# Layer 2 of a graph network kernel takes its one-hots from memory and raises to a power for two groups at once; layer 0 copies turned one-hots ahead of its exponential

## The chip, the cores and the metric

One NeuronCore of a Trainium2 chip runs the whole kernel in one launch. The time is the device time of that launch in microseconds, the median of several runs.

## The reference, cut to what matters

Four graph layers run one after the other on 6250 nodes with 106,250 edges (a source, a target and a weight each), with a normalisation ahead of each. Layer 0 is an attention over hyperedges, with sums over edges at one end and then at the other; layer 1 an MLP on both ends of an edge; layer 2 a gated message passing; layer 3 graph attention in two rounds. Layer 2 is the one that the change touches most:

```python
src_h = feat @ W_src + b_src
dst_h = feat @ W_dst + b_dst
se = src_h[edge_src]
de = dst_h[edge_dst]
h = gelu(se @ W1a + de @ W1b + b1)
h = gelu(h @ W2 + b2)
msg = _layernorm(h @ W3 + b3, ln_g, ln_b)
gate = jax.nn.sigmoid(gelu(se @ Wg1a + de @ Wg1b + bg1) @ Wg2 + bg2)
msg = gate * msg
upd = jax.ops.segment_sum(msg, edge_dst, num_segments=N)
return upd @ W_out + b_out
```

## The kernel before

The edges are sorted once by the block of 128 nodes that their target (and in a second order, their source) lies in. They are padded to 928 tiles of 128 edges; four tiles are a **group**, and there are NG = 232 groups. Every pass over the edges is a software pipeline over groups. Each engine has its own program, written out in full: in iteration j of `sweep`, a step with lag n works on group j - n, and `turn(j, u, n)` gives that group if it exists. The engines meet only through semaphores, whose counts are worked out in advance (`RAISED` says how often a group raises each of them in a pass). Nothing schedules: the order in the text is the order on the engine. `ORDER = "abafcdee"` lists the passes: a and b in the first half of layer 0 (b is its sum pass), a and f in the second half, c for layer 1, d for layer 2, e twice for layer 3. Between passes all engines meet (`meet`).

Rows of node tables are gathered by indirect DMAs that POOL issues, four per group (`rows_po`, L585). Sums over edges into nodes are matmuls with **one-hots**: a 128x128 matrix with a one where an edge belongs to a node of its block. Their turned form (transposed) spreads node values over edges. The one-hots of a group are 128x512 comparisons on VectorE (`onehot_ve`, L891, from `iof` and `LOW`, both in SBUF); `turn_pe` (L910) transposes them on TensorE, and `turned_ac` (L916) copies the result from PSUM. Pass b writes the source side's one-hots to memory, pass f the target side's, in 768 columns a group: 256 hold the turned form in bf16, 512 the plain form. Layer 1 (pass c) and f read them back on SP's queue in one transfer a group (`stream_sp`); layer 2 before the change builds its own. The sum of a group is read by `add_ve` (L884, L887), which adds two blocks to the accumulators at addresses that it takes from block numbers in memory: `blocks` (L565) loads them into registers on the queue of the engine.

Layer 2, pass d, for group g in iteration j of each engine: sv matmuls of the turned one-hots (lag 2, L1332), z on VectorE (lag 3, L1204), transposes and Gelu (lag 4, L1324, L1281, L1283), W2 (lag 5, L1318), Gelu (L1276) and the gate's product and sum (L1227, L1242), then W3 (lag 6, L1307), z3 = product + b3 (L1213), batch statistics (L1233, L1249), variance + eps (L1254), the gate's tanh (L1271); POOL raises the variance to -0.5 (`d_po`, L1187, 128x4); lag 7: VectorE makes scale and bias (L1221, L1222, L1237) and ScalarE scales z3 (L1293, four times); lag 8: sums (L897); lag 9: adds. The reciprocal root stands on POOL ahead of the gathers of iteration j:

```python
for j in range(NG + 6):
    if j >= 6:
        ...
        po.tensor_tensor(dRS[:, g % 2, :], dVE[:, g % 2, :], dPW, ALU.pow).then_inc(S.rs, 1)
    if j < NG:
        ...
        rows_po(po, p, 0, tab[256], dG, j)
```

## Time and profile before

| | us |
|---|---|
| median of 3 runs | 11944.33 (11938.95 to 11951.59) |
| profiled execution | 11948.37 |
| its span | 11946.6 |

Busy shares of the span: PE 73%, DVE 69%, POOL 66%, ACT 43%. The profile gives in its parts: the busy time of each engine, the same in slices of time, DMA queues, a chain of what ended last, and groups of instructions by line. A row of a group has the engine and line, what is written and read, the count after x, the busy time in us, the mean length of one in ns, and the idle time of the engine just before, with what released it ("issue": nothing that the profile shows). A row of the timeline has the start in us, the length in us, the engine and line. A row of the windows has the stretch, its length, then for PE, PEld, DVE, ACT and POOL the busy time with the number of instructions, then the granted clock of TensorE as a share of full speed, the DMA share, and GB/s. PE is the matmul side of TensorE, PEld its weight loads, DVE VectorE, ACT ScalarE, POOL GpSimd.

### The profile page before, as it was taken

To read this page: it belongs to the slowest core of one execution; us is meant where nothing else is said; L and a number is where in the kernel's file an instruction comes from. 1 tells how busy PE (TensorE), PEld (TensorE's weight loads), DVE (VectorE), ACT (ScalarE), POOL (GpSimd) and SP (SyncE) were. 2 spreads that over 40 slices of the span, in tenths; PEclk is the share of its full clock that TensorE was granted. 3 is DMA by queue.
4 is the path that set the end of the run, shared out by engine and by line. 5 is a ranking of instruction groups with operands and counts; after the bars stand their busy time and mean duration, and the time that the engine had idled before them with its cause. 6 is when DMAs were issued, how large, how long until landed. Compare 5 with 4: busy or idle time off the path is not lost. (4 is left out here: it accounts for less than half of the span.)

```text
span 11946.6 us, 191958 instructions
## 1 busy us (share of the span) xinstructions
PE 8708.9 (73%) x51661; PEld 7108.5 (60%) x51661; DVE 8225.6 (69%) x30197; ACT 5137.3 (43%) x14885; POOL 7921.6 (66%) x7887
## 2 busy tenths in 40 slices
PE   7797877788885887666654555689997677767776
PEld 5676777677764777544443555577776455444554
DVE  7655888755556777655554222499998688878888
ACT  3454444433333444322221111266665466646665
POOL 2333777677774777677764777288885577747775
PEclk7766677655555666665656666799999665666656
DMA  1112222255552222377763444233332444434443
GB/s 16 7 19 38 54 54 54 56 126 126 128 129 58 54 54 54 97 202 203 202 168 93 131 132 131 79 89 88 88 88 68 124 135 134 136 105 136 134 135 114
DMA packets 612550, 1206.43 MB, mean 101 GB/s; under 512 B 185426, under 2 KB 298544, under 8 KB 610992
## 3 DMA queue, kind: packets, MB, share of 16 engines
q0 software_dynamic: 282368, 575.57, 22.4%
q1 hardware_dynamic: 288768, 523.78, 13.7%
q10 hardware_dynamic: 40368, 94.82, 2.1%
q8 instruction: 452, 7.41, 0.3%
q14 instruction: 594, 4.87, 0.1%
HBM read 958.79 MB, written 234.74 MB: 100 GB/s over the span
## 5 line engine op out<-in xcount | busy, mean ns | idle before, releaser
L585 POOL DMA_INDIRECT WK<-tab,IDX x4640 | 4608.4, 993 | 1736.2 <-issue 1391.7
L1388 POOL DMA_INDIRECT B<-tab,IDX x1856 | 1774.1, 956 | 844.8 <-issue 503.7
L897 PE MATMUL PS<-WK 128*128 128x129 f32 x5568 | 1140.8, 368 | 628.4 <-ACT WK L1134 500.5
L897 PEld LDWEIGHTS PS<-WK 128*128 128x128 f32 x5568 | 992.4, 267 | 719.4 <-ACT WK L1134 550.4
L1407 DVE TENSOR_REDUCE WK<-PS 128x4 f32<-128x1024 f32 x928 | 1131.4, 1220 | 184.0 <-PE PS L1533 181.9
L1518 ACT ACTIVATE B<-B 128x33 f32<-128x33 f32 x5568 | 1211.2, 308 | 7.9
L585 POOL DMA_INDIRECT H<-tab,IDX x928 | 901.9, 972 | 345.8 <-issue 256.2
L816 ACT ACTIVATE WK<-WK 128x128 f32<-128x128 f32 x1856 | 592.6, 390 | 1242.1 <-DMA WK<-tab,IDX 1230.0
L1566 PEld LDWEIGHTS PS<-B,H 128*128 128x128 f32 x3712 | 815.4, 329 | 273.9 <-issue 268.1
L1566 PE MATMUL PS<-B,H 128*128 128x132 f32 x3712 | 874.7, 428 | 78.5 <-DVE ACC L1420 78.3
L1533 PE MATMUL PS<-B 27*128 27x512 bf16 x1856 | 729.8, 505 | 118.8 <-DVE WK L1407 114.3
L453 POOL DMA_INDIRECT pieces<-WK,B x208 | 342.4, 1646 | 703.3 <-ACT WK L441 405.4
L845 PE MATMUL PS<-B 128*128 128x130 f32 x3712 | 797.2, 383 | 1.5 <-DVE B L776 1.5
L860 PEld LDWEIGHTS PS<-WK,B 128*128 128x128 f32 x3712 | 661.6, 267 | 176.0 <-issue 173.7
L860 PE MATMUL PS<-WK,B 128*128 128x2 f32 x3712 | 642.1, 295 | 128.6 <-DVE WK L773 127.5
L1120 DVE TENSOR_TENSOR WK<-PS,WK 128x512 f32<-128x512 f32 x232 | 160.5, 692 | 816.1 <-DMA WK<-tab,IDX 816.1
L845 PEld LDWEIGHTS PS<-B 128*128 128x128 f32 x3712 | 708.8, 283 | 2.4 <-DVE B L776 2.3
L645 PE MATMUL PS<-B,WT 128*15 128x512 bf16 x464 | 268.3, 578 | 569.6 <-ACT B L667 399.7
L387 PEld LDWEIGHTS PS<-B,WK 128*128 128x128 f32 x3328 | 530.9, 252 | 183.2 <-issue 181.4
L387 PE MATMUL PS<-B,WK 128*128 128x64 f32 x3328 | 529.5, 336 | 121.6 <-ACT WK L441 115.3
L1134 ACT ACTIVATE WK<-WK 128x512 f32<-128x512 f32 x232 | 146.6, 632 | 1028.3 <-DVE WK L1120 1028.3
L838 PE MATMUL PS<-WT,B 128*128 128x128 bf16 x1856 | 228.4, 262 | 451.9 <-ACT B L821 426.8
(426 smaller groups left out, 20454.5 us busy)
## 6 DMA issues: line engine op xcount, KB each, us to landing
H<-onehots SPq DMA_DIRECT2D x232, 768.0 KB
B<-onehots SPq DMA_DIRECT2D x232, 384.0 KB
onehots<-B ACTq DMA_DIRECT2D x232, 384.0 KB
WK<-onehots SPq DMA_DIRECT2D x232, 384.0 KB
WK<-tab,IDX POOLq DMA_INDIRECT x4640
onehots<-WK SPq DMA_DIRECT2D x232, 256.0 KB
onehots<-B SPq DMA_DIRECT2D x232, 128.0 KB
B<-tab,IDX POOLq DMA_INDIRECT x1856
```

The lines of the kernel that those rows point to most:

```text
L387: mm = pe.matmul(PS[:, 4 + x % 2, 64 * (t // TC):64 * (t // TC) + 64], OHL[x % 2][:, t, :], PROD[x % 2][:, t, :, :].rearrange("p i w -> p ...
L453: po.indirect_dma_start(out=recd[o], out_offset=bass.IndirectOffsetOnAxis(ap=ROWI[:, o, 2 * k + q:2 * k + q + 1], axis=0), in_=OUT[x % 4][ ...
L585: po.indirect_dma_start(out=G[:, g % n, k, :], out_offset=None, in_=table, in_offset=bass.IndirectOffsetOnAxis(ap=IDX[:, idx, t:t + 1], ax ...
L816: i = ac.activation(aXR[:, r % 4, k, :], aN1[:, 128 * k:128 * k + 128], ACT.Identity, bias=aG[:, r, k, 128:129])
L845: mm = pe.matmul(aAG(r, k // 2), aOH[:, r, k, :], aR[:, r % 2, k, 0:130], start=k % 2 == 0, stop=k % 2 == 1)
L860: mm = pe.matmul(as2[:, k, :], aOT[:, r % 4, 128 * k:128 * k + 128], aY[:, r % 2, k // 2, 1:3], start=True, stop=True)
L897: mm = pe.matmul(AG(r, k // 2), OH[:, r, k, :], R[:, r % 2, k, 0:129], start=k % 2 == 0, stop=k % 2 == 1)
L1388: po.indirect_dma_start(out=eG[:, g % 4, k, :], out_offset=None, in_=tab[TW3], in_offset=bass.IndirectOffsetOnAxis(ap=IDX[:, o, t:t + 1], ...
L1407: ve.tensor_reduce(eM2[:, g, b:b + 2, 2 * i:2 * i + 2, 1] if isinstance(g, int) else eM2[:, bass.ds(g, 1), b:b + 2, 2 * i:2 * i + 2, 1].re ...
L1518: i = ac.activation(eR[:, q, k, 33 * h:33 * h + 33], eG[:, r, k, 33 * h:33 * h + 33], ACT.Copy, scale=eEX[:, r, 4 * k + h:4 * k + h + 1])
L1533: mm = pe.matmul(PS[:, b + h, :], eSEL[:, b + h, :], eET[:, r, 512 * i:512 * i + 512], start=True, stop=True)
L1566: mm = pe.matmul(eAG(k // 2), eSTo[:, r, k // 4, 128 * (k % 4):128 * (k % 4) + 128], eR[:, r % 2, k, 0:132], start=k % 2 == 0, stop=k % 2 ...
```

## The change

Layer 2 no longer builds its one-hots. Pass f has left them in memory, and SP streams them in two transfers a group, into four buffers each (`d_sp`): the turned form as it is read by ScalarE, which widens it from bf16 to f32 (lag 1, where it copied from PSUM before), and the plain form six groups later, for the sums. VectorE's `onehot_ve` and TensorE's `turn_pe` are gone from the pass. POOL raises to the power for two groups in one instruction (128x8), at every second iteration. Scale, bias and the scaling move from lag 7 to 8, the sums from 8 to 9, the adds from 9 to 10; some small buffers are deeper. In pass b, ScalarE's two copies of the turned one-hots (group j - 1) stand ahead of the exponential (group j - 3).

```diff
-    "d": dict(oh=1, pt=1, ot=1, sv=1, z=1, zt=1, h1=1, mm=1, h2=1, p3=1, gp=1, gl=1, th=1, z3=1, bn=1, mv=1,
+    "d": dict(ot=1, sv=1, z=1, zt=1, h1=1, mm=1, h2=1, p3=1, gp=1, gl=1, th=1, z3=1, bn=1, mv=1,
...
-KEPT = {"a": 0, "b": 48, "f": 16, "c": 16, "d": 0, "e": 32}
+KEPT = {"a": 0, "b": 48, "f": 16, "c": 16, "d": 16, "e": 32}
...
             def body(j, u):
-                if f := turn(j, u, 3):
-                    g, r = f
-                    ac.wait_ge(S.p2, at.p2 + g + 1)
-                    ac.wait_ge(S.r, at.r + g - 3)
-                    ac.activation(bEX[:, r % 4, :], bDD[:, r % 2, :], ACT.Exp).then_inc(S.ex, 1)
                 if f := turn(j, u, 1):
                     g, r = f
                     kept(ac, 1, g, r)
                     ac.wait_ge(S.pt, at.pt + g + 1)
                     ac.activation(bTBt[r % 4], PS[:, r % 2, 0:256].bitcast(BF16), ACT.Copy).then_inc(s_kt, 1)
                     turned_ac(ac, at, g, r, bOT, r % 2)
+                if f := turn(j, u, 3):
+                    g, r = f
+                    ac.wait_ge(S.p2, at.p2 + g + 1)
+                    ac.wait_ge(S.r, at.r + g - 3)
+                    ac.activation(bEX[:, r % 4, :], bDD[:, r % 2, :], ACT.Exp).then_inc(S.ex, 1)
                 if f := turn(j, u, 2):
...
-        dOH, dOT, dR, dH2, dZ3 = room(fd, 8, 4, 128), room(fd, 2, 512), room(fd, 2, 4, 133), room(fd, 512), room(fd, 2, 512)
-        dBN, dMV = room(fd, 2, 4, 6), room(fd, 2, 4, 2)
-        dVE, dRS, dTH, dGW, dGT, dNM, dGL = (room(fd, 2, 4) for _ in range(7))
-        dPW = room(fd, 4)
+        dSTt = [room(fd, 256).bitcast(BF16) for _ in range(4)]
+        dSTo = room(fd, 4, 4, 128)
+        dOT, dR, dH2, dZ3 = room(fd, 2, 512), room(fd, 2, 4, 133), room(fd, 512), room(fd, 3, 512)
+        dBN, dMV = room(fd, 2, 4, 6), room(fd, 4, 4, 2)
+        dTH, dGW, dNM, dGL = (room(fd, 2, 4) for _ in range(4))
+        dVE, dRS, dGT = (room(fd, 4, 4) for _ in range(3))
+        dPW = room(fd, 2, 4)
         hf, xf = flat(H[:, :, :]), flat(X[:, :, :])
...
             for j in range(NG + 6):
-                if j >= 6:
-                    g = j - 6
+                g = j - 6
+                if g % 2 == 1 and g > 0:
                     po.wait_ge(S.mv, at.mv + g + 1)
-                    po.wait_ge(S.r, at.r + g - 1)
-                    po.tensor_tensor(dRS[:, g % 2, :], dVE[:, g % 2, :], dPW, ALU.pow).then_inc(S.rs, 1)
+                    po.wait_ge(S.r, at.r + g - 3)
+                    h = g % 4 - 1
+                    po.tensor_tensor(dRS[:, h:h + 2, :], dVE[:, h:h + 2, :], dPW, ALU.pow).then_inc(S.rs, 2)
                 if j < NG:
                     po.wait_ge(S.z, at.z + j - 3)
                     rows_po(po, p, 0, tab[256], dG, j)
@@ -1193,8 +1197,8 @@
...
-                z, w, l, f = turn(j, u, 6), turn(j, u, 7), turn(j, u, 5), turn(j, u, 0)
-                if x := turn(j, u, 9):
+                z, w, l = turn(j, u, 6), turn(j, u, 8), turn(j, u, 5)
+                if x := turn(j, u, 10):
                     add_ve(ve, at, 0, *x, AGd)
...
-                    qz = rz % 2
+                    qz, vz, sz = rz % 2, rz % 4, gz % 3
                     ve.wait_ge(S.p3, at.p3 + gz + 1)
-                    ve.wait_ge(S.rs, at.rs + gz - 1)
-                    ve.wait_ge(S.r, at.r + gz - 1)
-                    ve.tensor_tensor(by128(dZ3[:, qz, :]), by128(PS[:, 5, :]),
+                    ve.wait_ge(S.rs, at.rs + gz - 3)
+                    ve.wait_ge(S.r, at.r + gz - 2)
+                    ve.tensor_tensor(by128(dZ3[:, sz, :]), by128(PS[:, 5, :]),
                                      b3b.unsqueeze(1).broadcast_to([128, 4, 128]), ALU.add).then_inc(S.z3, 1)
                 if w:
                     gw, rw = w
-                    qw = rw % 2
-                    ve.wait_ge(S.rs, at.rs + gw + 1)
+                    qw, vw = rw % 2, rw % 4
+                    ve.wait_ge(S.rs, at.rs + gw - gw % 2 + 2)
                     ve.wait_ge(S.ag, at.ag + gw - 1)
                     ve.wait_ge(S.r, at.r + gw - 1)
-                    ve.tensor_copy(dR[:, qw, :, 128], dGT[:, qw, :])
-                    ve.tensor_tensor(dGW[:, qw, :], dGT[:, qw, :], dRS[:, qw, :], ALU.mult).then_inc(S.gw, 1)
+                    ve.tensor_copy(dR[:, qw, :, 128], dGT[:, vw, :])
+                    ve.tensor_tensor(dGW[:, qw, :], dGT[:, vw, :], dRS[:, vw, :], ALU.mult).then_inc(S.gw, 1)
                 if l:
                     gl, rl = l
                     ve.wait_ge(S.h1, at.h1 + gl + 1)
@@ -1230,11 +1234,11 @@
                 if z:
...
-                if f:
-                    onehot_ve(ve, at, 0, *f, dOH)
...
-                    ac.wait_ge(S.r, at.r + g - 1)
+                    ac.wait_ge(S.mm, at.mm + g - 1)
...
-                    turned_ac(ac, at, *f, dOT, 0)
-                if f := turn(j, u, 7):
+                    g, r = f
+                    streamed(ac, p, g, r)
+                    ac.wait_ge(S.sv, at.sv + g - 1)
+                    ac.activation(dOT[:, r % 2, :], dSTt[r % 4], ACT.Copy).then_inc(S.ot, 1)
+                if f := turn(j, u, 8):
                     g, r = f
                     q = r % 2
                     ac.wait_ge(S.nm, at.nm + g + 1)
                     ac.wait_ge(S.ag, at.ag + g - 1)
                     for k in range(4):
-                        i = ac.activation(dR[:, q, k, 0:128], dZ3[:, q, 128 * k:128 * k + 128], ACT.Identity,
+                        i = ac.activation(dR[:, q, k, 0:128], dZ3[:, g % 3, 128 * k:128 * k + 128], ACT.Identity,
                                           bias=dNM[:, q, k:k + 1], scale=dGW[:, q, k:k + 1])
                     i.then_inc(S.r, 1)
             meet(ac)
-            sweep(7, body)
+            sweep(8, body)
+
+        def d_sp(sp, p):
+            at, ring = raised_before(p)
+            for j in range(NG + 6):
+                if j < NG:
+                    sp.wait_ge(S.ot, at.ot + j - 3)
+                    sp.dma_start(dSTt[j % 4], oht[0][j, :, 0:256].bitcast(BF16)).then_inc(s_kd[j % 4], 16)
+                if j >= 6:
+                    g = j - 6
+                    sp.wait_ge(S.ag, at.ag + g - 3)
+                    sp.dma_start(dSTo[:, g % 4, :, :].rearrange("p k n -> p (k n)"), oht[0][g, :, 256:768]).then_inc(
+                        s_k0[g % 4], 16)
 
...
-                if f := turn(j, u, 1):
-                    turn_pe(pe, at, *f, upper(dOH), 0, 1)
-                if f := turn(j, u, 8):
-                    sum_pe(pe, at, *f, dOH, dR, AGd, 1)
+                if f := turn(j, u, 9):
+                    g, r = f
+                    pe.wait_ge(s_k0[r % 4], 32 * (NG // 4) + 16 * (g // 4 + 1))
+                    sum_pe(pe, at, g, r % 4, dSTo, dR, AGd, 1)
...
             meet(sp)
+            d_sp(sp, 5)
             meet(sp)
```

The rows that follow are the engines' programs in order: source line, operation, written and read tensor, shape. Lines behind the change are shifted by four or more. On VectorE in layer 2, before, from the variance + eps (L1254) of one iteration into the next:

```order
L1254 TENSOR_SCALAR WK<-WK 128x4
L891 TENSOR_TENSOR WK<-iof,LOW 128x512
L565 TENSOR_LOAD BLK
L884 ISA
L884 TENSOR_TENSOR ACC<-ACC,PS 128x129
L887 ISA
L887 TENSOR_TENSOR ACC<-ACC,PS 128x129
L1204 TENSOR_TENSOR H<-PS,H 128x1024
L1213 TENSOR_TENSOR WK<-PS,WT 128x512
```

And after:

```order
L1258 TENSOR_SCALAR WK<-WK 128x4
L565 TENSOR_LOAD BLK
L884 ISA
L884 TENSOR_TENSOR ACC<-ACC,PS 128x129
L887 ISA
L887 TENSOR_TENSOR ACC<-ACC,PS 128x129
L1208 TENSOR_TENSOR H<-PS,H 128x1024
L1217 TENSOR_TENSOR WK<-PS,WT 128x512
```

Only the comparison that makes the one-hots (L891) is gone; the load of block numbers (L565) and the address arithmetic (ISA) for the add stay between the variance and the add.

On POOL in layer 2, with the semaphores that an instruction waits for, before:

```order
L1187 TENSOR_TENSOR WK<-WK 128x4 [waits p_r,p_mv]
L585 DMA H<-tab,IDX 128x256 [waits p_z]
L585 DMA H<-tab,IDX 128x256 x3
L1187 TENSOR_TENSOR WK<-WK 128x4 [waits p_r,p_mv]
L585 DMA H<-tab,IDX 128x256 [waits p_z]
L585 DMA H<-tab,IDX 128x256 x3
```

And after:

```order
L1191 TENSOR_TENSOR WK<-WK 128x8 [waits p_r,p_mv]
L585 DMA H<-tab,IDX 128x256 [waits p_z]
L585 DMA H<-tab,IDX 128x256 x3
L585 DMA H<-tab,IDX 128x256 [waits p_z]
L585 DMA H<-tab,IDX 128x256 x3
```

The power stands ahead of every second group's four gathers, with twice the columns.

On ScalarE in pass b, one iteration and a half, before (L970 is the exponential, L975 and L916 the copies, L649 the copy of the bit form):

```order
L970 ACTIVATE WK<-WK 128x4 [waits p_r,p_p2]
L975 ACTIVATE B<-PS 128x512 [waits p_pt,k_kept1]
L916 ACTIVATE WK<-PS 128x512 [waits p_sv,p_pt]
L649 ACTIVATE B<-PS,WT 15x512 [waits k_bits]
L970 ACTIVATE WK<-WK 128x4 [waits p_r,p_p2]
```

And after, where L970 is the copy and L976 the exponential:

```order
L970 ACTIVATE B<-PS 128x512 [waits p_pt,k_kept3]
L916 ACTIVATE WK<-PS 128x512 [waits p_sv,p_pt]
L976 ACTIVATE WK<-WK 128x4 [waits p_r,p_p2]
L649 ACTIVATE B<-PS,WT 15x512 [waits k_bits]
L970 ACTIVATE B<-PS 128x512 [waits p_pt,k_kept0]
```

The exponential has moved from ahead of the two copies to behind them.

## Rows read from the trace of the kernel before

**Rows 1.** Windows inside pass b, layer 1 and layer 2.

```profile
2400.00:3600.00 1200.00, 1009.85 (x4684) 845.32 (x4683) 614.28 (x2454) 407.25 (x892) 928.26 (x892) 0.53 0.56 127
6450.00:7450.00 1000.00, 572.60 (x3986) 519.72 (x3982) 253.19 (x597) 125.72 (x199) 757.46 (x797) 0.69 0.45 131
7800.00:9100.00 1300.00, 1182.78 (x7295) 956.56 (x7296) 1234.90 (x4294) 857.33 (x1931) 1058.55 (x1074) 1.00 0.30 88
```

**Rows 2.** Groups of instructions of POOL in layer 2, 7800 to 9100 us.

```profile
L1187 POOL TENSOR_TENSOR WK<-WK 128x4 f32<-128x4 f32 x215 | 224.2, 1043 | 5.0
```

**Rows 3.** Timeline of POOL in layer 2, one group.

```profile
8400.00 1.04 POOL L1187 TENSOR_TENSOR WK<-WK 128x4 f32<-128x4 f32 x1
8401.23 1.02 POOL L585 DMA_INDIRECT H<-tab,IDX  x1 [0.19 <-issue]
...
8405.08 0.95 POOL L585 DMA_INDIRECT H<-tab,IDX  x1 [0.31 <-issue]
8406.07 1.04 POOL L1187 TENSOR_TENSOR WK<-WK 128x4 f32<-128x4 f32 x1
```

**Rows 4.** Timeline of DVE in layer 2, the same group time.

```profile
8400.27 0.68 DVE L1213 TENSOR_TENSOR WK<-PS,WT 128x512 f32<-128x512 f32 x1
8401.08 0.17 DVE L1221 COPY WK<-WK 128x4 f32<-128x4 f32 x1
...
8401.23 0.73 DVE L1227 TENSOR_TENSOR X<-X 128x512 f32<-128x512 f32 x1
...
8403.79 0.24 DVE L1254 TENSOR_SCALAR WK<-WK 128x4 f32<-128x4 f32 x1
8403.94 0.68 DVE L891 TENSOR_TENSOR WK<-iof,LOW 128x512 f32<-128x512 f32 x1
8404.55 0.29 DVE L884 TENSOR_TENSOR ACC<-ACC,PS 128x129 f32 x1
```

**Rows 5.** Timeline of PE and ACT in layer 2, the same time.

```profile
8399.92 1.16 PE L897 MATMUL PS<-WK 128*128 128x129 f32 x8 [0.51 <-ACT WK L1293]
8401.10 1.10 PE L1318 MATMUL PS<-X,WT 128*128 128x512 f32 x2
...
8402.24 0.69 ACT L1276 ACTIVATE WK<-PS,WT 128x512 f32<-128x512 f32 x1 [1.97 <-PE PS L1318]
...
8402.47 1.89 PE L1332 MATMUL PS<-B,WK 128*128 x8
...
8403.82 0.60 ACT L916 ACTIVATE WK<-PS 128x512 f32<-128x512 bf16 x1
...
8404.20 1.05 PE L1307 MATMUL PS<-WT,WK 128*128 128x128 f32 x8
...
8404.29 1.64 ACT L1293 ACTIVATE WK<-WK 128x128 f32<-128x128 f32 x4
```

**Rows 6.** Timeline of DVE at the end of layer 2's pass.

```profile
9149.54 0.29 DVE L884 TENSOR_TENSOR ACC<-ACC,PS 128x129 f32 x1 [0.54 <-issue]
...
9152.11 0.17 DVE L1221 COPY WK<-WK 128x4 f32<-128x4 f32 x1
...
9157.91 0.16 DVE L1221 COPY WK<-WK 128x4 f32<-128x4 f32 x1
```

**Rows 7.** The power at 49 columns, in the normalisations; shortest, median, longest in ns.

```profile
L546 POOL TENSOR_TENSOR WK<-WK x6: 8162/8194/8792, 1050.1 to 9245.0; 128x49 f32<-128x49 f32 x6
```

**Rows 8.** Groups of instructions in pass b, 2400 to 3600 us.

```profile
L585 POOL DMA_INDIRECT WK<-tab,IDX x892 | 928.6, 1041 | 272.0 <-issue 259.9 <-DVE WK L939 12.2
...
L645 PE MATMUL PS<-B,WT 128*15 128x512 bf16 x223 | 132.8, 595 | 163.2 <-ACT B L975 162.0
```

**Rows 9.** A ScalarE instruction that reads SBUF, in layer 1, from the groups of the page.

```profile
L1134 ACT ACTIVATE WK<-WK 128x512 f32<-128x512 f32 x232 | 146.6, 632 | 1028.3 <-DVE WK L1120 1028.3
```

**Rows 10.** Timeline of DVE and POOL in pass b, one gather and a multiplication.

```profile
2808.37 0.69 DVE L939 TENSOR_TENSOR WK<-WK 128x512 f32<-128x512 f32 x1
2808.52 1.37 POOL L585 DMA_INDIRECT WK<-tab,IDX  x1 [0.30 <-issue]
```

More of the change, by code:

```diff
@@ L1246, in body @@
                     ve.wait_ge(S.th, at.th + gz + 1)
-                    ve.tensor_scalar(dGT[:, qz, :], dTH[:, qz, :], 0.5, 0.5, ALU.mult, ALU.add)
+                    ve.tensor_scalar(dGT[:, vz, :], dTH[:, qz, :], 0.5, 0.5, ALU.mult, ALU.add)
                     for k in range(4):
-                        i = ve.bn_aggr(dMV[:, qz, k, :], dBN[:, qz, k, :])
+                        i = ve.bn_aggr(dMV[:, vz, k, :], dBN[:, qz, k, :])
                     i.then_inc(S.mm, 1)
@@ L1253, in body @@
                     ve.wait_ge(S.mm, at.mm + gz + 1)
-                    ve.tensor_scalar(dVE[:, qz, :], dMV[:, qz, :, 1], EPS, None, ALU.add).then_inc(S.mv, 1)
-                if f:
-                    onehot_ve(ve, at, 0, *f, dOH)
+                    ve.tensor_scalar(dVE[:, vz, :], dMV[:, vz, :, 1], EPS, None, ALU.add).then_inc(S.mv, 1)
             for i in range(NGR - 4, NGR):
@@ L1260, in d_ve @@
             meet(ve)
-            sweep(9, body)
+            sweep(10, body)
         def d_ac(ac, p):
```

6 lines of the change are left out of this document (3 added, 3 removed).

## The prediction

> **What bounds the kernel now.** I read the windows by stage first, to see which engines are full in the two stages that the change touches. In the part of layer 2 that lies between its ramps, 1300 us of it, PE is busy 1182.78, DVE 1234.90, POOL 1058.55, and the granted clock is 1.00 [rows 1]. Busy shares don't decide it there, since three engines are above 80%. So I read POOL's own timeline next. The reader is to see that a group takes five instructions in a fixed rhythm: the power at 8400.00, four gathers of which the first starts at 8401.23 and the last at 8405.08, the next power at 8406.07, with 0.19 to 0.31 us of idle time before a gather that only issue explains, and none before the power [rows 3]. The grouped row says the same of all of them: 215 powers of 1043 ns with 5.0 us idle ahead of them in total [rows 2]. POOL waits for nobody, so it is full, at a group time of (8406.07 - 8400.00) = 6.07; over the window, 1300 us hold 215 groups, 6.05 us each (6.06 by first and last start; I use 6.06).
>
> Two more loops are nearly as long. VectorE: the add of b3 ends at 8400.95, and the copy of the gate (L1221) starts at 8401.08, 0.04 after the power has ended (8400.00 + 1.04) and 0.13 after the add, where the following instructions start before their predecessor has ended [rows 3, 4]. So VectorE gives some 0.2 us a group to the power. ScalarE and TensorE: from the start of the first Gelu at 8402.24 to the end of the four scale instructions (8404.29 + 1.64) are 3.69 us; the sum matmuls then start (0.51 idle, released by that instruction), and 1.18 later the W2 matmul, which lasts 1.10 and releases the next Gelu [rows 5]. That is 3.69 + 0.06 + 1.18 + 1.10 + 0.04 = 6.07, the whole group time, but W2 also waits for VectorE's add, which ended only 0.15 before it started. All three loops move in step, and the one without slack is POOL's.
>
> In the first sum pass of layer 0, POOL is full as well: 892 gathers, 928.6 busy and 272.0 idle, of 1200 us [rows 8]. PE waits there 163.2 us for ScalarE's copy (L645), which costs nothing while POOL sets the pace.
>
> **Layer 2, the power for two groups.** One instruction on 128x8 takes the place of two on 128x4. The trace has this operation at two widths: 1043 ns for 4 columns [rows 2] and 8194 ns for 49 [rows 7]. The line through both is 0.41 us + 0.159 us a column, so 8 columns take 1.68 us. Bounds: proportional to the columns, 2 x 1.04 = 2.08; by the rate of the wide one with nothing fixed, 8 x 8194/49 = 1.34; and nothing but a fixed cost, 1.04. I take 1.68, since the two rows leave a fixed part of 0.4 and a much larger part per column. The Trainium skill (GPSIMD Engine Reference, section 3.1) puts an element of a two-input operation at about 2.6 cycles of that engine, which would make columns almost free, and 8 of them hardly dearer than 4; the two rows speak against it for a power, with 159 ns a column.
>
> POOL's two groups then are: power to first gather 1.23 + (1.68 - 1.04) = 1.87; the next three starts 3.85 later in all, as now; the second group without a power, four starts 1.25 apart, as in the pass of layer 1 where nothing else runs on POOL (797 instructions in 1000 us, [rows 1]); and 0.99 from the last gather to the next power [rows 3]. Sum 1.87 + 3.85 + 5.00 + 0.99 = 11.71, or 5.86 a group, 0.20 less than now.
>
> **Layer 2, the one-hots streamed.** VectorE loses L891, 0.68 us. I cost that at almost nothing. The instruction behind it, the add to the accumulator (L884), needs block numbers that the queue loads from memory, and the queue gets to them once L1254 is started: L1254 starts at 8403.79, L884 at 8404.55, 0.76 later, and L891 lies in that gap [rows 4]. The end of the stage shows the same iteration without L891, since no one-hots are left to build: the gap stays, L884 at 9149.54 with 0.54 of idle time that issue explains [rows 6]. Two whole iterations there without it, with VectorE never waiting for another engine, are 9157.91 - 9152.11 = 5.80 us [rows 6]. So VectorE's own loop is 5.80 to 5.85, before and after, and that is a floor.
>
> PE loses four transposes; they lie between L1307 and the sums, where it waits 0.51 for ScalarE anyway [rows 5], so nothing is gained. ScalarE copies from SBUF in place of PSUM: L1134, from SBUF, takes 632 ns [rows 9] against 0.60 for L916 [rows 5], so +0.04 in its loop. That loop without VectorE's hold on W2: W2 has started 0.02 after the sums' modelled end, while L1307 starts 0.16 ahead of the end of L1332 [rows 5], so some 0.18 of it is wait, and 6.07 - 0.18 + 0.04 = 5.93 bounds the loop from above; the same sum with the W2 matmul itself shortened by its cold start (its weights could load during the sums) is about 5.87, an estimate. I take 5.88 for the group: POOL's 5.86 and 0.02 for loops that touch, as now.
>
> The two streams per group go on SP's queue, 384 KB, as in layer 1, where the DMA share is 0.45 and the starts on POOL keep their 1.25 us [rows 1]. Layer 2 now has 0.30; with the stream it stays under 0.6. I cost it at nothing. Its cover: a transposed block is asked for when the copy four groups before it is done, about 17 us ahead. SP waits for the sums of group g-4 before the second form, and the next first form is queued behind that; the sums named are two iterations old by then, so it isn't late. The extra stage (sums one group later, adds one later) lengthens the end: one more power width, 0.64, and one more set of scale instructions, 1.64 [rows 5], some 2 us.
>
> Sum: 232 x (6.06 - 5.88) = 42 us, less 2 = 40 faster.
>
> **Layer 0, copies ahead of the exponential.** Nothing is added or removed. The copies no longer stand behind an exponential that waits for rows; PE's wait at L645 should go. The exponential now stands behind copies that wait for PE's transposes of two groups further on, but they are done about when the rows for it land. POOL's gathers are what all wait for, and I put the gain at 0. What could move is the lock in the next paragraphs, by up to 43 us either way.
>
> The sum is made against the profiled execution, 11948.4 us (span 11946.6): 11908.4. It is 4.0 above the median of 11944.33, so I predict 11905.
>
> **Rivals.**
> 1. The power costs in proportion, 2.08. POOL's pair is 12.11, as now; time 11944 + 2 = 11946. For it: the rows of 49 columns may be of another rhythm than short ones. Also here: the change doesn't reach the path at all.
> 2. The power's second half is nearly free (1.04 to 1.34). POOL falls to 5.54 to 5.69, and VectorE's 5.80 to 5.85 decides: 232 x 0.23 - 2 = 51 faster, 11893. VectorE idle would vanish and POOL show waits for L1254.
> 3. The port. In the pass of layer 0 a gather that starts 0.15 after a multiplication with two SBUF inputs (L939) takes 1.37 in place of 0.95 [rows 10]. In layer 2 the like instruction (L1227) and the first gather both start at 8401.23 [rows 3, 4], and that gather takes 1.02: a tie that POOL wins now. If VectorE wins it after the change, each pair costs 0.5 more, 0.25 a group, 58 us: 11963. Against it: both are still released by the end of the same power. The Trainium skill (SBUF - State Buffer, who interferes with whom) says that a VectorE instruction with two SBUF inputs and a GpSimd instruction that reads SBUF exclude each other, and whichever starts first holds the port. By that rule, the trace agrees in layer 0 (1.37 for 0.95), and the one-hots gone would be locks gone; in layer 2 the row shows no gather that L891 delays, so I count no gain. In layer 0, mean gathers of 1041 ns against 757.46/797 = 950 in layer 1 [rows 1, 8] cost 4 x 0.09 x 232 = 84 us; another phase could halve or add half of that, 42: 11863 or 11947.
> 4. The other side: TensorE's clock. Granted 1.00 in layer 2 at a busy share of 91%, but 0.53 in layer 0's sum pass at 84% and 0.69 in layer 1 [rows 1]. PE's 1182.78/215 = 5.5 us a group, less 0.4, is 5.1; at 0.69 it would be 7.4 and PE the bound: 232 x 1.34 = 310 slower, 12255. It decides from a clock of about 0.87 down (5.1/5.88). Against it: what is removed is small, and the shorter group packs the rest as densely.
>
> **How the numbers follow.** The case of the sum (5.86 to 5.93 a group, 11894 to 11917): 0.60. Rival 1: 0.12. Rival 2: 0.08. Lock in layer 2: 0.06. Clock: 0.03. Layer 0 off by more than 20 us, on top of the sum: 0.11, half each way. The range 11880 to 11946 takes in the sum's case with its neighbours, rivals 1 and 2, and leaves out the port, the clock and half of layer 0's. A measurement here tells 0.2%, 24 us, from no change, so below 11920 counts as faster: 0.60 x 0.95 + 0.08 + 0.05 = 0.70; slower (above 11968): the clock, part of the port, 0.06; the same: 0.24.
>
> **What the profile after would show.** Power instructions 116 of 1.68 us; starts of powers 11.7 to 11.8 apart; gathers in the second group 1.25 apart; an idle of about 0.6 ahead of L884 with "issue"; PE still waiting for ScalarE ahead of the sums; clock 1.00; in layer 0 no wait at L645 and the same 5.38 a group. I am wrong if the power's width is off by more than 0.2, if a gather in layer 2 is over 1.2 us, or if layer 0's mean gather moves by more than 20 ns.

## The result, and the profile after

The changed kernel takes 11871.4 us (median of 4 runs, 11866.9 to 11892.34) against 11941.85 (4 runs of the kernel before beside them), a ratio of 0.9943 (95% interval 0.9926 to 0.996): 70 us faster, where 39 were forecast. Its profiled execution took 11892.34 (span 11890.6), its slowest run; the kernel before had 11948.4 there.

The windows of the changed kernel, inside pass b, layer 1 and layer 2 (length, then PE, PEld, DVE, ACT and POOL busy, granted clock, DMA share, GB/s), answer to [rows 1]:

```profile
2400.00:3550.00 1150.00, 967.32 (x4550) 791.84 (x4550) 597.67 (x2387) 422.23 (x867) 886.05 (x867) 0.56 0.54 129
6450.00:7450.00 1000.00, 574.75 (x4006) 516.96 (x4004) 254.40 (x600) 126.36 (x200) 755.90 (x802) 0.70 0.46 132
7800.00:9000.00 1200.00, 1032.13 (x6120) 847.74 (x6120) 1051.18 (x3876) 801.10 (x1837) 961.18 (x919) 1.00 0.52 157
```

Layer 2 holds 204 groups in 1200 us, 5.88 us each, at a clock of 1.00. But look at the second window too: layer 1, which the change doesn't touch, has 802 gathers in its 1000 us, where it had 797.

Groups of instructions of the changed kernel in layer 2, 7800 to 9000 us, beside [rows 2, 4, 5]:

```profile
L585 POOL DMA_INDIRECT H<-tab,IDX x817 | 792.1, 970 | 236.9 <-issue 236.9
L1191 POOL TENSOR_TENSOR WK<-WK 128x8 f32<-128x8 f32 x102 | 170.3, 1670 | 2.2
L884 DVE TENSOR_TENSOR ACC<-ACC,PS 128x129 f32 x204 | 59.2, 290 | 110.9 <-issue 110.9
```

The power for two groups takes 1670 ns (1.68 forecast). The idle time ahead of L884, where the one-hots lay, is 110.9/204 = 0.54 us. POOL waits for no engine.

The timeline of POOL there, beside [rows 3]:

```profile
8401.48 1.67 POOL L1191 TENSOR_TENSOR WK<-WK 128x8 f32<-128x8 f32 x1
8403.34 1.02 POOL L585 DMA_INDIRECT H<-tab,IDX  x1 [0.19 <-issue]
8404.66 0.95 POOL L585 DMA_INDIRECT H<-tab,IDX  x1 [0.30 <-issue]
```

From the power to the first gather 1.86 (1.87 forecast), then eight gathers; the first is 1.02 long as before, so the tie with VectorE's product is still POOL's. The sixth is another matter. Over the pass it takes 1022 ns in the mean, where the undisturbed ones take 950: VectorE's product of the other group (L1231) starts 0.2 to 0.6 us ahead of it, mostly 0.5. (In the second execution of this kernel, below, it is the second gather behind the power in place of the sixth, with 1021 ns.) 14 gathers of the pass are over 1.2 us, 11 of them sixth ones; before there was one in all. The longest, with its product:

```profile
8715.40 0.69 DVE L1231 TENSOR_TENSOR X<-X 128x512 f32<-128x512 f32 x1
...
8715.58 1.34 POOL L585 DMA_INDIRECT H<-tab,IDX  x1 [0.30 <-issue]
```

Groups of the changed kernel in pass b, 2400 to 3550 us, beside [rows 8]:

```profile
L585 POOL DMA_INDIRECT WK<-tab,IDX x867 | 887.7, 1024 | 264.3 <-issue 253.9 <-DVE WK L939 10.4
...
L645 PE MATMUL PS<-B,WT 128*15 128x512 bf16 x217 | 127.5, 588 | 0.0
```

The wait at L645 is gone, and the mean gather is 1024 ns where it was 1041.

Where the time went is best read pass by pass. Each number below is the time in us from the start of the first gather of a pass to the start of its last (928 gathers), taken from the records of one profiled execution; the last column is from the first gather of layer 2 to the end of the execution.

| kernel | a | b | a again | f | c (layer 1) | d (layer 2) | d to the end |
|---|---|---|---|---|---|---|---|
| before | 1186.3 | 1248.3 | 1191.4 | 1226.3 | 1164.2 | 1398.0 | 4194.6 |
| changed | 1173.7 | 1230.5 | 1189.5 | 1234.6 | 1157.4 | 1359.3 | 4160.2 |
| difference | -12.6 | -17.8 | -1.9 | +8.3 | -6.8 | -38.7 | -34.4 |

Layer 2 gave what was forecast (-39). The other 31 us are 37 from passes a, b and c, of which the change touches only b, and 2 from the repetition of a, less 8 that f takes back. Behind layer 2 some of it is lost again: the gathers of layer 3 (L1388, L1405 changed) have a median of 955 ns for 952, and are 2545.6 us from first to last for 2539.1. (In this execution the part ahead of the first gather took 10 us longer, 1148.3 for 1138.0, and 1127.5 in another of the same kernel; it drifts.)

### The profile page after: what moved, and what is told of

It is laid out like the page before. It is cut to its first block and busy times, and to the rows that moved or that the text cites. A ratio compares the mean times of both kernels' runs of the same rounds, so it can differ in the third digit from the quotient of the medians.

```text
span 11890.6 us, 189871 instructions
## 1 busy us (share of the span) xinstructions
PE 8648.0 (73%) x50733; PEld 7039.9 (59%) x50733; DVE 8092.2 (68%) x29965; ACT 5150.1 (43%) x14885; POOL 7848.2 (66%) x7771
## 5 line engine op out<-in xcount | busy, mean ns | idle before, releaser
L1405 POOL DMA_INDIRECT B<-tab,IDX x1856 | 1782.6, 960 | 840.2 <-issue 504.3
L1120 DVE TENSOR_TENSOR WK<-PS,WK 128x512 f32<-128x512 f32 x232 | 160.5, 692 | 811.9 <-DMA WK<-tab,IDX 808.6
L387 PEld LDWEIGHTS PS<-B,WK 128*128 128x128 f32 x3328 | 538.5, 254 | 177.9 <-issue 175.7
L645 PE MATMUL PS<-B,WT 128*15 128x512 bf16 x464 | 267.8, 577 | 395.2 <-ACT B L667 392.5
L995 PEld LDWEIGHTS PS<-B,WK 128*128 128x128 f32 x1856 | 378.9, 303 | 265.9 <-issue 265.9
```

Source lines behind the costliest of these rows:

```text
L387: mm = pe.matmul(PS[:, 4 + x % 2, 64 * (t // TC):64 * (t // TC) + 64], OHL[x % 2][:, t, :], PROD[x % 2][:, t, :, :].rearrange("p i w -> p ...
L995: mm = pe.matmul(PS[:, 2 + r % 2, k:k + 1], bOT[:, r % 2, 128 * k:128 * k + 128], B2[:, bass.ds(v[k // 2], 1)], start=True, stop=True)
L1405: po.indirect_dma_start(out=eG[:, g % 4, k, :], out_offset=None, in_=tab[TW3], in_offset=bass.IndirectOffsetOnAxis(ap=IDX[:, o, t:t + 1], ...
```

## The experiments

Two questions: which part of the change gives what, and why do gathers outside layer 2 get shorter? For the second, the records of pass b give a first theory. In the kernel before, 306 gathers start less than 0.7 us after the start of a VectorE instruction with two SBUF operands (L891, L939). Grouped by that offset, they are longer than the undisturbed ones by these medians:

| offset, ns | 68 | 137 | 237 | 338 | 436 | 545 | 645 |
|---|---|---|---|---|---|---|---|
| before: number, ns longer | 26, 493 | 112, 425 | 35, 324 | 36, 226 | 33, 125 | 31, 16 | 33, 0 |
| changed: number, ns longer | 17, 490 | 98, 429 | 30, 338 | 35, 222 | 35, 136 | 41, 17 | 59, 0 |

So such a gather is held until 0.56 us after that instruction's start: in each column but the last, offset and lengthening of the kernel before add up to 561 to 564 ns. I call the sum of these lengthenings the **lock** of a pass: 84 us in pass b before, 73 changed.

Each set of experiments ran on a chip of its own, with the kernel before run in between; ratios are to that. "Pass b 1233.3" means the span of gathers as in the table above.

### The parts of the change

**The changed kernel again**, no edit.

> The changed kernel once more, to see how far its runs lie apart and what the passes outside the change do. Both theories: 65 to 75 us faster than before (ratio 0.994). Theory A (the order of the copies in layer 0 gives what layer 2 doesn't): pass b is 25 to 35 us shorter than before, and the first pass a is as before. Theory B (no edit gives it; POOL's gathers in passes that the change doesn't touch are shorter by chance, by the port and by a base length that differs between executions): the shortening is spread over passes a, b, f and c, 5 to 15 us each, with both signs from run to run.

11869.43 us, ratio 0.9937 (0.9923 to 0.995), which is 75 us; the medians are 86 apart. Pass b 1237.3, layer 2 1358.7, c 1157.3, and the first pass a 1165.2: all of it is there again. Theory A is out as it stands (a is 21 us shorter, b only 11), and so is B's "by chance": c has the same 7 us.

**Layer 2 alone**: pass b's order put back.

```diff
+                (exponential, lag 3)
                 (copies of the turned one-hots, lag 1)
-                (exponential, lag 3)
```

> Layer 2 as changed, layer 0's pass b in the old order. A: 39 us faster than before (0.9967), layer 2 at 5.88 us a group. B: the same 65 to 75 us as the full change.

11889.13, ratio 0.995 (0.9936 to 0.9964): 60 us. Layer 2 1358.6. Passes a and c are as short as in the changed kernel (1168.3, 1157.5), so they come with layer 2's part of the change.

**The order in pass b alone**: the same edit the other way, in the kernel before.

> Only the order of ScalarE's copies and exponential in pass b. A: 25 to 35 us faster (0.9975), with the mean gather of pass b down from 1041 ns by 30 ns. B: within 10 us of before.

11931.74, ratio 0.9981 (0.9972 to 0.999), 23 us faster. Pass b 1233.3 for 1248.3, with 69 us of lock for 84 and a mean gather of 1026 ns for 1042, half of what A forecast; the other passes are within 6 us of before. The forecast gain of 0 is refuted.

**The stream without the pair**: one power of 128x4 for each group, the rest of layer 2 as changed, pass b as before.

```diff
-                if g % 2 == 1 and g > 0:
+                if g >= 0:
...
-                    po.tensor_tensor(dRS[:, h:h + 2, :], dVE[:, h:h + 2, :], dPW, ALU.pow).then_inc(S.rs, 2)
+                    po.tensor_tensor(dRS[:, g % 4, :], dVE[:, g % 4, :], dPW[:, 0, :], ALU.pow).then_inc(S.rs, 1)
```

> Layer 2 with streamed one-hots and the later stages, but the power for one group at a time, 128x4; layer 0 in the old order. POOL then has five instructions a group again and sets 6.05 us a group: within 5 us of before by the mechanism of the prediction (power is the whole gain). The rival, that VectorE's one-hots or TensorE's transposes held the loops: 5.9 us a group, 35 us faster.

11998.55, ratio 1.0037 (1.0024 to 1.0051): slower than before. Layer 2 took 1424.9, 27 more than before. Its timelines of POOL and VectorE show the prediction's third rival at work, on the fourth gather of a group:

```profile
8406.80 1.42 POOL L585 DMA_INDIRECT H<-tab,IDX  x1 [0.30 <-issue]
...
8406.71 0.69 DVE L1230 TENSOR_TENSOR X<-X 128x512 f32<-128x512 f32 x1
```

The product starts 0.09 ahead of the gather, and the gather is 0.47 longer, 0.56 in all, as in pass b. 42 of the 232 fourth gathers, 18 in 100, take over 1.1 us. The power is held in the same way: 33 of 231 take more than 1.1 us, up to 1.57, where none did before. Gathers are 17 us longer in sum and powers 9.5, which is the 27. The rhythm of layer 2 decides whether a product falls ahead of a gather or a power; in the changed kernel it is one gather of a pair's eight, at a cost of some 8 us in the pass.

**The pair without the stream**: one-hots built by VectorE and turned by TensorE as before, the power for two groups.

```diff
+                if f:
+                    ve.tensor_tensor(dOH[:, g % 9, :, :], io4, low(0, g), ALU.is_equal).then_inc(S.oh, 1)
...
-                    streamed(ac, p, g, r)
-                    ac.activation(dOT[:, r % 2, :], dSTt[r % 4], ACT.Copy).then_inc(S.ot, 1)
+                    turned_ac(ac, at, *f, dOT, 0)
```

> Layer 2 with the power for two groups, but one-hots still built by VectorE and turned by TensorE (in 9 buffers, z3 in another place in memory); layer 0 in the old order. If the power is what layer 2 gained, and L891 lies in the shadow of the load of block numbers, layer 2 is at 5.88 us a group as with the streams, and the whole some 60 us faster than before, as the kernel with both parts of layer 2. Rival, that both parts are needed: VectorE with L891 is over its loop and layer 2 stays at 6.0 us or more.

11910.57, ratio 0.9967 (0.9955 to 0.9979), 39 us faster. Layer 2 1367.7; passes a and c short (1184.0, 1157.3). Its groups in layer 2, 7800 to 9000 us:

```profile
L585 POOL DMA_INDIRECT H<-tab,IDX x813 | 795.5, 979 | 235.7 <-issue 235.7
L1193 POOL TENSOR_TENSOR WK<-WK 128x8 f32<-128x8 f32 x101 | 168.7, 1670 | 2.2
L1264 DVE TENSOR_TENSOR WK<-iof,LOW 128x512 f32<-128x512 f32 x202 | 137.7, 682 | 0.0
```

The rival is out, and so is the forecast of 60 us: layer 2 runs at 5.92 us a group (powers 11.84 apart in the mean). POOL is full here too, and its gathers are 979 ns against 970 with the stream. So in layer 2 the pair is worth 30 us, and the stream 9 more by taking away one-hots that hold gathers (10 us of lock by L1264). The prediction had costed VectorE's 0.68 us at almost nothing; as VectorE time that is right.

### The 8 ns of passes a, b and c

The undisturbed gather is 952 ns in passes a, b and c before, and 944 in the changed kernel. This view groups the instructions of one line in layer 1, 6450 to 7450 us, shortest, median and longest in ns; before, then changed:

```profile
L585 POOL DMA_INDIRECT WK<-tab,IDX x797: 947/952/964, 6449.7 to 7449.3; - x200
```

```profile
L585 POOL DMA_INDIRECT WK<-tab,IDX x802: 940/944/965, 6449.8 to 7449.8; - x161
```

The repetition of a, and f, have 944 in both. 928 gathers by 8 ns are 7.4 us a pass, 22 for the three. On the usual chips all kernels with the power of 128x8 have 944 there, those with 128x4 have 952. The first idea was POOL's program, which is 113 rows shorter with the pair.

**Padding**: 116 writes of one column (128x1) on POOL behind layer 2, in the changed kernel and in the kernel before.

```diff
             d_po(po, 5)
             meet(po)
+            for _ in range(116):
+                own(po, "po", po.memset(WT[:, 1399:1400], 0.0))
```

> The changed kernel with 116 small memsets on POOL, in a stretch after layer 2 where POOL is idle, so that its program is as long as before the change. Theory P (the length of a gather on POOL, 944 or 952 ns in passes that the change doesn't touch, goes with where POOL's program lies or how long it is): the first pass a, b and c go back to 952 ns a gather, and the whole is 20 to 35 us slower than the changed kernel. Rival: it stays at 944 ns and the time is the same.

> The kernel before with the same 116 memsets. Theory P: the length of the program is another one again, so the gathers may go to 944 ns in pass a, b and c (20 to 35 us faster) or stay; the rival: 952 ns and the time of before.

Changed and padded: 11877.9, ratio 0.9936 (0.9923 to 0.9949), still 944 ns. Before and padded: 11949.55, 1.0003 (0.9994 to 1.0012), still 952.

**Padding in place**: in the changed kernel, such a write behind two waits long met, where each second power stood.

```diff
+                elif g >= 0:
+                    po.wait_ge(S.mv, at.mv + g)
+                    po.wait_ge(S.r, at.r + g - 3)
+                    own(po, "po", po.memset(WT[:, 1399:1400], 0.0))
```

> What it is: the changed kernel, in which POOL gets in every other group of layer 2, where the power of one group stood before, a write of one column (128x1) of an unused tile behind two waits that have long been met. POOL's program is then 4,179 rows long where before has 4,174 and the changed kernel 4,061, each row of layer 2 at about the place it has in before. Theory P (the undisturbed gather of passes a, b and c takes 944 ns in place of 952 because of the length of POOL's program or of the place of its instructions): it is 952 ns here again, and passes a, b and c are 5 to 8 us longer each than in the changed kernel. Rival Q (it is something that the 128x8 power itself brings, or its tiles): 944 ns stays.

11878.71 (2 runs), ratio 0.9935 (0.9912 to 0.9958), still 944. Length and place in POOL's program are not it.

**Two narrow powers** in place of the wide one, tiles, waits and streams as changed.

```diff
-                    po.tensor_tensor(dRS[:, h:h + 2, :], dVE[:, h:h + 2, :], dPW, ALU.pow).then_inc(S.rs, 2)
+                    po.tensor_tensor(dRS[:, h, :], dVE[:, h, :], dPW[:, 0, :], ALU.pow).then_inc(S.rs, 1)
+                    po.tensor_tensor(dRS[:, h + 1, :], dVE[:, h + 1, :], dPW[:, 1, :], ALU.pow).then_inc(S.rs, 1)
```

> What it is: the changed kernel with two powers of 128x4 one behind the other on POOL, every second group, in place of one of 128x8; tiles, waits, streams and order as in the changed kernel. Settles more of where the shorter undisturbed gather of passes a, b and c (944 ns for 952) comes from: the padded kernels spoke against the length of POOL's program. If it comes with the instruction of 8 columns, the gather is 952 ns here, as in the kernel with one power per group; if it comes with what goes with pairing (tiles of four groups, one stage more in layer 2's sweep), it stays 944 ns. Layer 2: two powers are 2.09 us for 1.67, so 6.1 us per group for 5.88, the gathers of layer 2 from first to last about 1405 us and the whole about 11,920.

> Two powers of 128x4 one behind the other in place of one of 128x8, once more on another chip. In the first run the undisturbed gather of passes a, b and c was 952 ns (944 in the kernels with one 128x8 power on the same chip), and that of the passes behind layer 2 fell to 944. If that goes with the kernel, both are so here again; if it was that chip, a, b and c are 944 ns. Layer 2: about 1405 us from first gather to last, 6.1 us per group; the whole, with 8 ns more per gather in three passes, 11,920 to 11,945 us.

The first run fell on an odd chip (below), the second gave 11928.59, ratio 0.998 (0.9971 to 0.999), layer 2 1394.9, 10 us under its forecast. On both chips a, b and c have 952 ns, and the repetition of a and f 944. (On the odd chip the kernels with the power of 128x8 have 947 in all five of these passes, not the 944 that the second expectation gives them.) The second run, layer 1:

```profile
L585 POOL DMA_INDIRECT WK<-tab,IDX x797: 947/952/968, 6449.8 to 7449.5; - x200
```

So the 8 ns go with the kernel, not with the chip, and not with the deeper tiles or the later stages; nothing is left that differs but the form and number of the power instructions, which run after the passes in question. What carries it back to them isn't found. Layer 3, behind the powers, moves too, and not in step: a median of 952 before, 955 changed, 944 with two narrow powers.

### Taking the lock away

**One SBUF operand in pass b.** The one-hots and the product of 128x4x128 are made by four instructions each, with one SBUF operand and a number per partition.

```diff
-            ve.tensor_tensor(OH[:, r, :, :], io4, low(o, g), ALU.is_equal).then_inc(S.oh, 1)
+            for k in range(4):
+                i = ve.tensor_scalar(OH[:, r, k, :], iof[:, :], LOW[:, o, 4 * g + k:4 * g + k + 1], None, ALU.is_equal)
+            i.then_inc(S.oh, 1)
...
-                    ve.tensor_tensor(bR[:, q, :, 0:128], bG[:, r % 4, :, 0:128],
-                                     bEW[:, q, :].unsqueeze(2).broadcast_to([128, 4, 128]), ALU.mult).then_inc(S.r, 1)
+                    for k in range(4):
+                        i = ve.tensor_scalar(bR[:, q, k, 0:128], bG[:, r % 4, k, 0:128], bEW[:, q, k:k + 1], None, ALU.mult)
+                    i.then_inc(S.r, 1)
```

> The changed kernel, where in pass b VectorE makes the one-hots (L891) and the product with the weights (L939) by four instructions each that read one tensor from memory and take the other operand as a scalar per partition. If the exclusion between a VectorE instruction with two inputs from SBUF and a gather on POOL is what makes pass b's gathers 1030 ns long, they fall to 944 to 955 ns, the pass from 1235 to about 1165 us, and the kernel is 70 us faster than the changed one, 1.2% faster than before. The rival (memory traffic of the streams that pass b writes makes them long): 1020 to 1040 ns as now, no gain.

11803.71, ratio 0.9887 (0.987 to 0.9904). Pass b is 1163.0. Its timelines of POOL and VectorE, to set beside [rows 10]:

```profile
2807.61 0.96 POOL L585 DMA_INDIRECT WK<-tab,IDX  x1 [0.30 <-issue]
...
2807.47 0.87 DVE L942 TENSOR_SCALAR WK<-WK 128x128 f32<-128x128 f32 x4
```

The gather starts 0.14 after the product's first piece, as the one of [rows 10] did at 0.15 after the whole product, and is 0.96 long where that took 1.37. The same holds for all: 184 gathers of pass b start less than 0.5 us after the first of four such pieces, and in steps of 100 ns their medians are 0 to 37 ns over the undisturbed length (60 ns for the 32 that start 0.7 to 0.8 us after it). All gathers of the pass together are 5 us over it.

The pieces are also shorter than what they replace, 0.3 us for 0.69, so this run alone leaves open whether the second SBUF operand holds a gather or the length does. Layer 1 of the kernel before settles it. Its VectorE instruction L1120 has the length and width of the product, but one operand from PSUM and one from SBUF:

```profile
L1120 DVE TENSOR_TENSOR WK<-PS,WK 128x512 f32<-128x512 f32 x199 | 137.7, 692 | 696.5 <-DMA WK<-tab,IDX 696.5
```

113 gathers of that pass start less than 0.6 us after the start of one; in every step of 100 ns their median is 952, and the longest of all is 961. So length doesn't do it; two operands from SBUF do.

**The same with the old order**, exponential ahead of the copies.

> What it is: the kernel with one-input one-hots and products in the first sum pass of layer 0 (11,803.71 us, pass b 1163.0 us), with ScalarE's exponential back ahead of its copies of turned one-hots. Theory L (the order that the change gives ScalarE in that pass gains only by moving VectorE's two-operand instructions off the starts of the gathers): with no such instructions left the order is worth nothing: pass b 1163 us within 3 us, the whole 11,795 to 11,815 us. Rival S (the order shortens a chain that the gathers wait for, ring slots given back later in the old order): pass b 15 us or more longer, about 1178 us, and the whole about 11,820.

11801.44, ratio 0.9873 (0.9855 to 0.9892), pass b 1161.7. In pass b, 2400 to 3450 us:

```profile
L585 POOL DMA_INDIRECT WK<-tab,IDX x838 | 795.0, 949 | 255.4 <-issue 247.2 <-DVE WK L942 8.2
L645 PE MATMUL PS<-B,WT 128*15 128x512 bf16 x210 | 124.0, 591 | 109.3 <-ACT B L978 107.7
```

This separates the two things that the order did. PE's wait at L645 is back with 109 us, and the pass is no longer for it: that wait costs nothing. Without the lock the order is worth nothing, so its gain went through the lock, as theory L had it; rival S is out.

**One SBUF operand in all passes of layer 0**: also L755 and L776 in a, L654 and L1031 in f.

> What it is: the changed kernel with every one-hot and every product of 128x4x128 that VectorE makes out of two SBUF operands in layer 0 (L654, L755, L776, L891, L939, L1031) made by four instructions with one SBUF operand and a number per partition. In pass b alone this took the gathers' first-to-last from 1229.5 to 1237.3 us down to 1163.0. Theory L (the gathers of layer 0 lose their time above the undisturbed issue length to VectorE instructions with two SBUF operands that start in the same half microsecond): pass f (1229.6 to 1240.1 us in the changed kernels) falls to about 1160 as pass b did, pass a and its repetition lose their lock sums of 8 to 34 us, mostly in the first pass (1164 to 1182 down to about 1160), and the whole comes to 11,690 to 11,740 us, ratio to before about 0.980. Rival W (VectorE in pass a is busy 4.2 of 5.1 us per group; the four pieces cost about 0.25 us more than the one, twice, and VectorE becomes what the gathers wait for there): passes a and a2 get longer, above 1200 us each, and the whole is 11,750 or more. Rival N (in pass f it was something else, such as the table stream or the kept tiles): f stays at 1230 and the whole at about 11,780.

11802.75, ratio 0.9873 (0.9854 to 0.9892), no better. Pass f fell from 1235.2 to 1162.6 and the repetition of a from 1188.2 to 1180.0, but the first pass a went from 1164.2 to 1233.4. There, 1140 to 2373 us:

```profile
L585 POOL DMA_INDIRECT WK<-tab,IDX x919 | 868.3, 945 | 354.9 <-issue 219.9 <-DVE B L782 135.0
```

No gather is held, and POOL waits 135 us for the product instead: a gather needs its buffer back, and VectorE has it for longer. Some of that falls into idle time that was there anyway (357 us between the gathers in all, where it is 282 with only pass b's pieces), so 75 us of it are paid. Theory L held for pass f, rival W for the first pass a alone, rival N is out.

**One SBUF operand in b and f** (pass a as changed), and **in b, f and a's one-hots** (L755), each twice, since the first time fell on the odd chip.

> What it is: the changed kernel with the one-hots and products of the passes b and f of layer 0 (L891, L939, L654, L1031) made in four pieces with one SBUF operand each, and pass a as in the changed kernel. Making all of them so gave 11,802.75 us, no better than pass b alone (11,803.71), although pass f fell from 1235.2 to 1162.6 us: in that run's first pass a the gathers took 1233.4 us where 1164.2 stood, with 135 us of waits for VectorE's product. Theory W (that was VectorE, busy 4.2 of 5.1 us per group of pass a, on which the eight pieces add 0.5 us): with pass a left alone both gains add up: b and f about 1163 us each, pass a 1164 to 1182, its repetition 1190, the whole about 11,735 us (11,720 to 11,755). Rival M (the length of the first pass a moves for a cause of its own, from run to run, and the one-input pieces of passes b and f bring it on): a is 1210 us or more here too, and the whole is near 11,780.

> The kernel with one-input pieces in passes b and f once more. In its first run the chip was one on which the kernel before itself took 15,087.74 us (11,941 to 11,958 elsewhere), its engines standing for about 4.5 us at every second group of pass a with what the trace calls remote; that run can't speak of the gathers' locks. On a chip where before takes about 11,950 theory W stands as written: b and f about 1163 us each, the whole about 11,735 us (11,720 to 11,755). Rival M: the first pass a at 1210 us or more, the whole near 11,780.

> What it is: as the kernel with one-input pieces in passes b and f, and in pass a the one-hots (L755) too in four pieces, the product (L776) left in one. The one-hots carry most of pass a's lock (11 to 20 us of 16 to 30). Theory W: VectorE gets 0.25 us of work per group more in place of 0.5, which it has room for: no 100 us of waits for it, the first pass a and its repetition come to 1165 to 1175 us, the whole is 10 to 25 us under the kernel with b and f alone. Rival W2 (any added work on VectorE in pass a is paid, since its chain from a table row to the product is what gives the ring slot back): pass a 20 to 40 us longer than there, the whole no better or slower.

> The kernel with one-input pieces in passes b and f and for the one-hots of pass a once more, for the same reason. Theory W: the first pass a and its repetition 1165 to 1175 us, the whole 10 to 25 us under the kernel with b and f alone. Rival W2: pass a 20 to 40 us longer than there, the whole no better or slower.

On a usual chip, b and f give 11740.94, ratio 0.9827 (0.9813 to 0.9841): 1.7% under the kernel before and 1.1% under the changed one. a 1164.7, b 1163.0, f 1170.5, both forecast within 8 us. In pass f, 5000 to 6000 us, where the kernel before has gathers of 1024 ns in the mean:

```profile
L585 POOL DMA_INDIRECT WK<-tab,IDX x792 | 752.1, 950 | 248.9 <-issue 238.1 <-DVE WK L1037 10.8
```

With a's one-hots too it is 11750.98, ratio 0.9834 (0.9821 to 0.9847), no gain: the repetition of a gets shorter (1170.8 for 1189.8), the first pass longer (1193.8 for 1164.7), with the product left in one piece now holding 219 gathers for 30 us (5 gathers for 2 us with b and f alone). Making only one of two instructions harmless took lock away in the repetition (31 to 8 us) and brought more to the first pass, where the other now falls ahead of gathers. Of the two rival readings for pass a, W2 ("no better") came out, though by the lock and not by waits for VectorE: the idle time between the gathers is the same 282.5 us in both kernels.

**The odd chip.** There the kernel before took 15087.74 us, b and f 15763.45 (ratio 1.0446, 1.0422 to 1.047), b, f and a's one-hots 15752.96 (1.0439, 1.042 to 1.0459), the two narrow powers 15587.15 (1.033, 1.0303 to 1.0356). The list of waits of the b and f kernel in its first pass a there, 1146 to 2900 us (total, times, longest):

```profile
ACT B L823 <- remote: 518.1, 114, 16.4
DVE WK L725 <- remote: 504.7, 113, 7.0
```

VectorE and ScalarE stand 4.5 us at a time at every second group for something that the trace can't name; no list of waits elsewhere has that row. On this chip POOL isn't the bound, so its runs say nothing of the lock, and the numbers of the others don't hold there. What it is was not tried.

## Why the prediction was right and wrong

- **Layer 2, the power's width**: right. 1.68 was worked out from 4 and 49 columns, 1670 ns measured. Proportional cost (rival 1) and a free second half (rival 2) are out.
- **Layer 2, 5.88 a group**: right, 5.88, but in part by luck. POOL's own 5.86 was sound. The 0.02 on top was put in for "loops that touch", and no loop touched: POOL's powers waited 2.2 us in all. What filled its place is one gather of the pair's eight, held by VectorE's product, 0.07 a pair. The "two whole iterations" of 5.80 that gave VectorE's floor [rows 6] are one; the one before it, from 9146.05 to 9152.11, has no one-hots either and takes 6.06. No run was bound by that floor, so it stays untested. The sum said 40 us with the ramps, the gathers say 38.7, and layer 2 to the end 34.4, since layer 3 gives 6 back.
- **One-hots streamed at almost nothing**: right in sign, 9 us off. The step said that no row shows a gather that L891 delays in layer 2; in the rhythm of the pair some are (10 us of lock).
- **The rival of the port in layer 2**: on the first gather, where it was looked for, it did not happen in the changed kernel. It did on another, the sixth or the second, at some 8 us, and 14 gathers over 1.2 us are a sign that the prediction had named as one of being wrong. In the kernel with the stream alone it cost 27 us. The chance of 0.06 was on a real mechanism. **The clock** stayed at 1.00.
- **Layer 0, "I put the gain at 0"**: the step that failed, by size. Its two halves were right: the wait at L645 went, and is worth nothing. But the same paragraph said that the lock could move, and took the middle. Pass b has 5.30 us a group, where "the same 5.38" was to be seen. The lock moved to one side: 83 to 93 us of lock in pass b in five executions with the old order, 62 to 80 in six with the new one, so the order is worth some 15 to 20 us (23 by the times of the order alone).
- **Passes that the change doesn't touch**: a second term that failed, put at nothing without a reason. They gave 15 us (a and c), and b another 7, through 8 ns a gather. No row shown of before tells it, and the cause is open.
- The sum with what was measured: 39 in layer 2, some 15 by the order, 22 by the shorter gathers, less 6 in layer 3, 70 together; 70 and 75 (by the ratio of 0.9937) were measured. That they agree so well is luck, since the lock of a and f moves by 10 us either way from one execution to the next.

The Trainium skill (SBUF - State Buffer, "Who interferes with whom") has the rule by which this is to be read: two SBUF inputs contend with a GpSimd instruction that reads SBUF, and one input doesn't, outside VectorE's two-port modes. By that rule, the runs agree: with one operand the lock went from 73 us to 5 in pass b. The same section infers that a `tensor_tensor` does not stall the making of DMA descriptors; here it lengthens the gather that issues a DMA, by up to 0.5 us, and the measurement decides. The Trainium skill (SBUF - State Buffer, "SBUF: two separate sides") also says that the first to start gets the shared pair for the whole instruction. Here an instruction of 0.69 us holds a gather until 0.56 us after its start, and the trace doesn't show why 0.56.

## What to carry to other kernels

Where an engine is full, ask what lengthens its instructions, not only what it waits for: a mean of 1041 ns beside a median of 952 on POOL was 84 us in one pass, in no list of waits, and four one-operand instructions in place of a two-operand one took it away for some 0.2 us more, each, of an engine that had room. Where that engine has no room the gain is lost to a wait, and where several instructions take turns in the lock, replacing one of them can move the lock to another: in the two executions of pass a it gained 19 us in one and lost 29 in the other. If a mechanism is known to be worth tens of us and a change moves the phase between its two engines, its range belongs in the forecast's own range, not in a rival's small chance.

## What was unexpected of the hardware

- A gather on POOL that starts x after the start of a VectorE instruction with two SBUF operands (0.69 us long) is longer by 0.56 us - x, in passes a, b and f and in layer 2 alike; pieces of 128x128 in f32 with one SBUF operand and a number per partition (0.3 us each) do next to nothing to it (5 us in a pass). An instruction of the same 0.69 us with one of its operands from PSUM does nothing (113 gathers, none over 961 ns).
- Such an instruction holds a power on POOL as it holds a gather: 1.57 us for 1.04 at most, in the kernel with the stream alone.
- The power on POOL costs 0.41 us and 159 ns a column at 4, 8 and 49 columns.
- The undisturbed gather of one pass is 944 or 952 ns by a difference in another pass that runs later, on all of the usual chips tried. On the odd one it was 944, 947 or 952 by kernel and pass.
- One chip of those used ran the kernel before in 15088 us in place of 11950, and changes that gain 1.7% elsewhere lost 4.5% there.
